# A small residual convolution network: statistics by four 32-row products, image 1 loaded behind the first weights, 18 warm-up products

## What is computed

```python
def _gn(v, G=32, eps=1e-05):
    g = v.reshape(B_, G, C_ // G, H_, W_)
    m = jnp.mean(g, axis=(2, 3, 4), keepdims=True)
    s = jnp.var(g, axis=(2, 3, 4), keepdims=True)
    return ((g - m) / jnp.sqrt(s + eps)).reshape(v.shape)

x = x + _L0_conv_ref(_gn(x), ...)   # 12 convolutions with shortcuts, 2 transposed ones
```

## Time and profile before

| | us |
|---|---|
| median of 3 runs (lowest, highest) | 89.16 (89.05, 89.54) |
| the profiled execution's own time | 89.39 |
| its span in the trace | 87.6 |
| TensorE busy, share of the span | 81.0, 92% |
| VectorE, ScalarE, GpSimd busy | 56.6, 44.9, 27.2 |

### The profile page before, as it was taken

The page is one execution under the profiler, slowest core; times in us unless marked ns, Lnnn a source line. Parts: engine busy times, 40 slices in busy tenths (PEclk is TensorE's granted clock), DMA queues, the critical chain, the costliest instruction groups (busy, mean ns, idle before and its releaser), DMA issues.

```text
span 87.6 us, 1478 instructions
## 1 busy us (share of the span) xinstructions
PE 81.0 (92%) x513; PEld 72.4 (83%) x513; DVE 56.6 (65%) x165; ACT 44.9 (51%) x98; POOL 27.2 (31%) x43
## 2 busy tenths in 40 slices
PE   5999999999999999999999999999999999998800
PEld 3777999998877889999988777999999999686500
DVE  5659999799889696422253658899656766211840
ACT  6006214678555056555521149799999988001400
POOL 7200051799950000444451000100389000600230
PEclk9999999999999999999999999999999999999995
DMA  1988930032657106640000000000000000000084
GB/s 22 257 251 250 322 126 0 0 99 66 171 127 265 32 0 159 200 127 0 0 0 0 0 0 4 0 0 0 7 0 0 0 0 0 0 0 7 0 304 178
DMA packets 4183, 6.51 MB, mean 74 GB/s; under 512 B 464, under 2 KB 2128, under 8 KB 4176
## 3 DMA queue, kind: packets, MB, share of 16 engines
q1 hardware_dynamic: 4032, 6.29, 23.8%
q10 hardware_dynamic: 144, 0.13, 0.5%
HBM read 5.37 MB, written 1.05 MB: 73 GB/s over the span
## 4 chain that ended last, share of the span: by engine, by line
PE 84%; DMA 6%; SPq 2%; ACT 2%; issue 1%; POOLq 1%; DVE 1%
PE psum L853 78%; DMA raw<-e0b0c_in 6%; PE psum L887 3%; PE psum L1032 2%; SPq L454 1%; POOLq L175 1%; ACT w_e0b0c L537 1%; PE psum L1076 1%; SPq L458 0%; ACT result L626 0%; ACT shared L623 0%; DVE odd L770 0%; DVE last L768 0%; PE psum L880 0%; PE psum L873 0%
## 5 line engine op out<-in xcount | busy, mean ns | idle before, releaser
L506 POOL TENSOR_TENSOR odd<-relu,odd 128x363 fp32r<-128x363 f32 x12 | 13.5, 1146 | 15.5 <-ACT odd L578 15.5
L853 PE MATMUL psum<-shared,w_e0b0c 128*128 128x364 f32 x72 | 12.5, 331 | 0.1
L781 DVE SCALAR_TENSOR_TENSOR relu<-psum,inside 128x363 f32<-128x363 f32 (+1 forms) x16 | 8.1, 510 | 6.6 <-PE psum L853 5.1
L853 PEld LDWEIGHTS psum<-shared,w_e0b0c 128*128 128x128 f32 x72 | 11.9, 188 | 0.5 <-issue 0.4
L853 PE MATMUL psum<-shared,w_e0b1c 128*128 128x364 f32 x72 | 12.2, 329 | 0.0
L853 PEld LDWEIGHTS psum<-shared,w_e0b1c 128*128 128x128 f32 x72 | 12.1, 188 | 0.1
L853 PE MATMUL psum<-odd,w_e0b0c 128*128 128x512 f32 x48 | 11.6, 400 | 0.0
L853 PE MATMUL psum<-odd,w_e0b1c 128*128 128x512 f32 x48 | 11.6, 400 | 0.0
L853 PEld LDWEIGHTS psum<-odd,w_e0b1c 128*128 128x128 f32 x48 | 9.1, 189 | 2.2
L853 PEld LDWEIGHTS psum<-odd,w_e0b0c 128*128 128x128 f32 x48 | 9.1, 189 | 2.2
L578 ACT ACTIVATE odd<-relu 128x363 fp32r<-128x363 f32 x12 | 6.1, 506 | 6.6 <-DVE relu L781 6.6
(11 more groups left out here) (125 smaller groups left out, 126.0 us busy)
## 6 DMA issues: line engine op xcount, KB each, us to landing
x_sb<-x_in SPq DMA_DIRECT2D x4, 160.0 KB, 3.9
raw<-e0b0c_in SPq DMA_DIRECT2D x2, 256.0 KB, 5.2
raw<-e0b1c_in SPq DMA_DIRECT2D x2, 256.0 KB, 5.4
raw<-e1b1c_in SPq DMA_DIRECT2D x2, 256.0 KB, 2.7
raw<-e2b1c_in SPq DMA_DIRECT2D x2, 256.0 KB, 2.8
raw<-e1b0c_in SPq DMA_DIRECT2D x1, 448.0 KB, 3.9
raw<-e2b0c_in SPq DMA_DIRECT2D x1, 448.0 KB, 3.2
x_sb<-x_in SPq DMA_DIRECT2D x2, 192.0 KB, 3.9
```

The lines of the kernel that those rows point to most:

```text
L506: pool.tensor_tensor(split_of(piece, 1), fp32_of(piece), split_of(piece, 0).bitcast(F32), ALU.subtract).then_inc(lo_ready, 1)
L781: last = dve.scalar_tensor_tensor(out=target, in0=sums, scalar=0.0, in1=mask, op0=ALU.max, op1=ALU.mult)
L853: last = pe.matmul(target, w, moving, start=(first and n == 0), stop=(final and n == len(terms) - 1), skip_group_check=skip)
```

## The change

There are three edits. The masked copies and the mask go: `sum_stats` now multiplies, for each quarter q, the 32 rows of `same_channel` with the 32 rows of `stats` of that quarter, into a PSUM bank of its own (banks 4 to 7, 18 columns each), and `bn_aggr` reads the four banks. SP waits for the first weights to have landed before it issues x of image 1; all of its later loads stand behind that wait. The first batch of warm-ups has 18 products in place of 22, and warm-ups write bank 3 in place of bank 6.

```diff
-WARM_UP = [22, 14]
+WARM_UP = [18, 14]
+STATS_BANKS = [4, 5, 6, 7]
...
-        quad_mask = sb("quad_mask", [P, 4])[:]
...
                 if k == 0:
+                    sp.wait_ge(w_loaded[0], 16)
                     load_x(1)
...
-                step(last)
-
-                dve.tensor_tensor(spread[:, image], stats[:, image].unsqueeze(1).to_broadcast([P, 4, VALUES]),
-                                  quad_mask.unsqueeze(2).to_broadcast([P, 4, VALUES]),
-                                  ALU.mult).then_inc(stats_spread, 1)
+                last.then_inc(stats_ready, 1)
...
-                dve.bn_aggr(moments[:, image], psum[:, BANKS - 1, 0:4 * VALUES]).then_inc(moments_ready, 1)
+                dve.bn_aggr(moments[:, image], psum[:, STATS_BANKS[0]:STATS_BANKS[3] + 1, 0:VALUES]).then_inc(moments_ready, 1)
...
-            dve.memset(quad_mask, 0.0)
...
-            for q in range(4):
-                last = dve.memset(quad_mask[CH * q:CH * q + CH, q:q + 1], 1.0)
-            step(last)
...
-                pe.wait_ge(stats_spread, image + 1)
+                pe.wait_ge(stats_ready, image + 1)
                 pe.wait_ge(const_loaded, 16)
-                pe.matmul(psum[:, BANKS - 1, 0:4 * VALUES], same_channel[:, 0:P],
-                          spread[:, image].rearrange("p q s -> p (q s)"),
-                          start=True, stop=True).then_inc(stats_summed, 1)
-
-            def warm_up(count, bank=BANKS - 2):
+                for q in range(4):
+                    of_q = slice(CH * q, CH * q + CH)
+                    last = pe.matmul(psum[:, STATS_BANKS[q], 0:VALUES], same_channel[of_q, 0:P], stats[of_q, image],
+                                     start=True, stop=True)
+                last.then_inc(stats_summed, 1)
+
+            def warm_up(count, bank=STATS_BANKS[0] - 1):
```

More of the change, by code:

```diff
@@ L235, in build @@
         norm_step = sem("norm_step")
-        stats_spread = sem("stats_spread")
+        stats_ready = sem("stats_ready")
         stats_summed = sem("stats_summed")
@@ L444, in build @@
         eye = spare[:, 4 * P:5 * P]
-        spread = spare[:, 5 * P:5 * P + IMAGES * 4 * VALUES].rearrange("p (i q s) -> p i q s", i=IMAGES, q=4)
         block = ctx.enter_context(nc.Block())
```

## The result

The changed kernel takes **89.96 us** (median of 11 executions, 89.66 to 90.70), the kernel before 89.41 beside it (89.05 to 89.59). The ratio is 1.0084, with a 95% interval of 1.0061 to 1.0106: slower by over half a per cent. The profiled execution belongs to the first group (own time 89.66, span 87.9, against 89.39 and 87.6). Every ratio leaves out executions over 1.5% above the fastest of their kernel or in a slower state of the chip, which in the experiments are three of e1, six of e4 and one of e11, at 115.34.

What follows compares the result with a forecast made beforehand. TensorE's unbroken products from 8.25 us were taken as the bound. Start 0.45 earlier less 0.06 gives 0.39, image 1 limits it to 0.40; forecast gain 0.35, 89.39 - 0.35 = 89.04 (88.8 against the median), range 88.5 to 90.0.

Steps and rivals of the forecast that it cites:

- The earlier start: TensorE's first product of the first stage: start 0.45 us earlier than 8.25, with the statistics read 0.48 earlier.
- the estimate of 0.65: Image 0's four statistics products on TensorE: 0.65 us from their start to the reader, in place of 0.58.
- The last two rivals: Statistics products on TensorE: no faster than copy and one product, 89.1, chance 0.08; loads not overlapping, 89.9, chance 0.03.
- the last rival: Image 0's four products on TensorE: loads do not overlap, eight passes take 1.7 us, 89.9; chance 0.03.
- the term E: End of image 1's statistics on VectorE: W + 4.2, bounds W + 4.0 and W + 4.4; in time up to 10.4.
- W: Time at which the first weights have landed, image 1 held back: taken as 5.8 us, bounds 5.3 and 7.49.
- 10.4 - E: Gain limit at the GpSimd step from image 1's statistics: 6.2 - W, 0.40 us; the gain is the smaller of 0.39 and this.
- The first rival: Image 1 too late at L651 on VectorE, then GpSimd and TensorE wait: 89.8 at W = 6.8, 90.5 at 7.49; chance 0.25.
- That image 1 slows the first weights: DMA queue: nearly all first weights could have moved by 5.2; a last piece ran until 7.49 while mostly image 1 went by.
- The clock rising later: Rival at TensorE's warm-ups: hole from 4.90 to 5.15 delays the clock, start 0.35 later plus 0.5, 90.0; chance 0.12.
- Four products for image 1: TensorE in the first stage: four hold it 0.24 us in place of 0.18 for one, -0.06, leaving a gain of 0.39.
- the dec0 step: Profile row used to price the four products: eight passes in 0.50 us, next products 0.24 after them, at the higher clock.

Runs made afterwards that it cites:

- e1: The changed kernel without SP's wait for the first weights; four products and 18 warm-ups stay: 90.36 us, ratio 1.0069 to the kernel before.
- e4: The kernel before with 18 warm-ups in place of 22 and nothing else: 90.23 us, ratio 1.0004.
- e11: The changed kernel with 20 warm-ups and all later loads held until image 1's third part has landed: 89.44 us, ratio 1.0017 to the kernel before.
- e6: The changed kernel, wait included, with 20 warm-ups in place of 18: 89.62 us, ratio 1.0045 to the kernel before.
- e3: The changed kernel without SP's wait and with 22 warm-ups in place of 18: 89.56 us, ratio 1.0030 to the kernel before.
- e8: The kernel before with four 32-row statistics products for image 1 only: 89.65 us, ratio 1.0041.
- e2: The kernel before with SP's wait for the first weights alone added: 89.90 us, ratio 1.0078.
- e10: The changed kernel with 20 warm-ups and image 1 issued when image 0's third part has landed: 89.31 us, ratio 0.9996 to the kernel before.
- e9: The kernel before with four products for image 0 only, 20 warm-ups, image 1 issued when image 0's third part has landed: 89.05 us, ratio 0.9977.
- e5: The kernel before with 20 warm-ups in place of 22 and nothing else: 89.25 us, ratio 0.9995.

## Why the prediction was wrong

It forecast a gain of 0.35, and the medians show a loss of about 0.55. By its own steps:

- **The earlier start came out as forecast, in part by luck.** Reader at 5.77 (forecast 5.84, to be seen between 5.7 and 6.0), first product at 7.70 (7.80), with the step from reader to rows unchanged. But the first statistics product started at 5.29 in place of 5.15, and four products to their reader took 5.77 - 5.29 = 0.48 in place of 0.65: TensorE had reached 2.4 GHz by then, which the prediction did not count on, and the two errors cancel. At 1.2 GHz the estimate of 0.65 holds, as e6 shows with 6.14 - 5.45 = 0.69. By that figure the reader of the changed kernel would have come at 5.98 and the first product near 7.9. The last two rivals (no faster, no overlap of loads) are out: eight loads are issued in 0.31 us, or 0.52 at 1.2 GHz (e6), in place of the 1.7 of the last rival, and the four products start within 0.02 us of one another (5.29 to 5.31), so they run side by side.
- **The step that failed is the term E, the end of image 1's statistics.** The landing of the first weights, W, came at 6.12, within the bounds and 0.32 above the 5.8 taken; with E = W + 4.2 as forecast that would still be a gain of 0.1. But E, with bounds of W + 4.0 and W + 4.4, is 10.92 - 6.12 = W + 4.8, above both. It was priced by the pace of image 0 "alone in the queue", and image 1 is not alone: SP sends 64 to 256 KB loads close behind it. The prediction named these loads and asked only when they themselves would land. Held back (e11), they leave 10.65 - 6.25 = 4.4, the upper bound; the other 0.2 is the choice of the middle. Image 0 was not alone either, since constants, first weights and image 1 stand behind it; why it kept its pace is not shown. With E = 10.92 its own formula, 10.4 - E, gives -0.5; the end of the long piece moved by 0.38. The first rival thus describes the profile, at W = 6.1 rather than 6.8 or 7.49, and the twelve executions of e6, which has no second group, all lie at 89.55 or above, where the kernel before has its median at 89.27 on that chip.
- **That image 1 slows the first weights was right.** With image 1 issued right behind them they landed between 6.6 (e3) and 7.66 (e8), in before at 7.49; with image 1 held until they had landed, at 6.12 (after), 6.13 (e2), 6.23 (e6) and 6.26 (e11), by SP's issue. So the wait does buy 0.4 to 1.5 us for the weights. Image 1's statistics end 0.8 later for it (10.92 against 10.13), and they had only 0.3 to give (10.4 against 10.13).
- **The clock rising later had 0.12 and happened in about half of the executions** (18 of 33 with 18 warm-ups by the two groups of times; e4's profile shows it, for after and e1 it follows from the groups that go with 20 or 22). Its price in the prediction was 0.35 + 0.5 = 0.85; the long piece of e4 is 1.13 late. The mistake was to treat it as one event that happens or not, on the ground that one profile shows the rise at one point. The profile of after hides it: in it the clock rose early, and its 14 warm-ups took 1.70 us in place of 2.05.
- **Four products for image 1 were costed at +0.06 and cost 0.22 to 0.30 more than the one** by the lengths of e1, e3, e8 and e10; alone, in e8, 0.29 of length and 0.37 of time. The row taken, the dec0 step, measures from the first of its products to a next product that has 32 rows as well (`32*128` in both lines). It holds no change of rows, and the price that is paid once was missing. The products themselves cost about what was said (0.17 to 0.22, against 0.15 for the one).

So of the 0.93 lost in the profiled execution some 0.25 goes to the small products, as in e10, and about 0.65 to image 1 (e2 alone: 0.57); less 0.55 at the start. The split is an estimate, since the wait of 0.34 for image 1 and the change of rows fall in the same place. The issue rule of the Trainium skill that the prediction cited ("DMA: Bandwidth & Descriptors", section "Rules for kernel authors") fits the outcome: the wait alone costs 0.6 to 0.7 us (e2), and issuing 1.5 us sooner brings 0.3 to 0.4 back (e10).

With all three losses mended the early start is still worth little: e9 gains 0.2 us in its median, where its profiled execution starts 0.41 earlier than before (7.84). Part of it goes to the wait of 0.44 that is left, and part of the 0.41 is the early rise of the clock in that profile (4.0 against 6.8); the rest was not traced.

## What to carry to other kernels

When a load is put behind a wait, price its landing with what is queued behind it, not only with what was ahead, and compare the new landing with the slack of its reader, here 0.3 us. Take the price of a small step from a row with the same neighbours: four products of 32 rows between full ones cost 0.2 us here that the row from dec0 did not show, and belong where TensorE waits anyway. Where a filler is cut so that a hole may open near the rise of the clock, count executions, not one profile; and compare two profiles only after looking where the clock rose in each.

## What the runs showed that was not expected

- Small products among full ones: 0.34 us from the first of four to the next full product, 0.56 for eight, and 0.23 to 0.24 of idle weight loading ahead of either; one full product takes 0.15 with none.
- With 20 or 22 warm-ups the clock rose between 3.8 and 7.0 in the profiles; with four fewer than before it rose beyond 9 in that of e4, and by the times late in 18 of 33 executions; with two fewer in none of 24 (e5, e6). The hole's length alone does not decide: e5 has one of 0.25 us at 5.5 and no second group, after has one of 0.20 at 5.1 and a second group. In the profiles of the quicker groups the clock was up before the hole (4.3 in e1) or by its end (after), in e4 it was not; but in e5 it was not either. What decides was not settled. The Trainium skill ("TensorE: Matmul & The Clock Gate", section "What's actually happening") warns that the number of products at the lower clock differs between executions of one kernel; this case agrees, and the difference is 1.1 us or more of the whole.
- Loads issued behind a load delay its last piece by 0.4 us (3.81 against 4.24 from the first issue), and loads of image 1 behind the first weights delayed these by 0.4 to 1.5.
